# B and C convolution channels of the first layer in one 128-partition tile

## The reference

```
proj = x @ W_in.T                       # 512 z | 640 xBC | 4 dt
xp = jnp.pad(xBC, ((0, 0), (D_CONV - 1, 0), (0, 0)))
xc = conv_b + sum((xp[:, k:k + L, :] * conv_w[:, k] for k in range(D_CONV)))
xc = jax.nn.silu(xc)
x_ssm, B_ssm, C_ssm = xc[..., :512], xc[..., 512:576], xc[..., 576:]
dt = jax.nn.softplus(dt_raw + dt_bias)
A = -jnp.exp(A_log)
y = _ssd(x_ssm, dt, A, B_ssm, C_ssm) + x_ssm * D[:, None]
...                                     # rms norm of y, times silu(z), @ W_out.T
```

## Time and profile before

| | us |
|---|---|
| median of three runs | 1829.97 |
| lowest and highest run | 1828.99, 1835.95 |
| span of the profiled execution | 1829.6 |

### The profile page before, as it was taken

The page is one execution under the profiler, slowest core; times in us unless marked ns, Lnnn a source line. Parts: engine busy times, 40 slices in busy tenths (PEclk is TensorE's granted clock), DMA queues, the critical chain, the costliest instruction groups (busy, mean ns, idle before and its releaser), DMA issues. The chain is left out here.

```text
span 1829.6 us, 26010 instructions
## 1 busy us (share of the span) xinstructions
PE 1590.3 (87%) x7554; PEld 1124.3 (61%) x7554; DVE 1362.5 (74%) x3565; ACT 1149.7 (63%) x2769; POOL 756.6 (41%) x2052
## 2 busy tenths in 40 slices
PE   5799999989857889977997889878779999999987
PEld 2555657465646667766786678756645556555554
DVE  6665757572359999999999999999644466776646
ACT  3333342412148999899989998999547565665630
POOL 3504224240136776777666776777410100001000
PEclk9789999999879889999999899998999999999989
DMA  5000000000200000000000000000000000000000
GB/s 229 1 1 1 1 1 1 1 1 0 76 35 1 1 1 1 1 1 1 1 1 1 1 1 1 1 1 1 1 0 1 1 1 1 1 13 1 13 0 23
DMA packets 6717, 19.23 MB, mean 11 GB/s; under 512 B 1072, under 2 KB 4144, under 8 KB 5296
## 3 DMA queue, kind: packets, MB, share of 16 engines
q1 hardware_dynamic: 6576, 17.58, 2.6%
HBM read 15.48 MB, written 2.10 MB: 10 GB/s over the span
## 5 line engine op out<-in xcount | busy, mean ns | idle before, releaser
L1349 DVE BATCH_NORM_STATS2 r_moments<-mem_arena 128x6 f32<-128x512 f32 x576 | 382.2, 682 | 4.4 <-ACT mem_arena L1632 4.3
L1632 ACT ACTIVATE mem_arena<-mem_arena,r_shift 128x256 f32<-128x256 f32 x792 | 351.3, 514 | 32.9 <-POOL r_shift L1540 32.9
L1700 PE MATMUL r_bank<-arena,r_wT 128*128 128x256 f32 x1024 | 228.2, 381 | 7.2 <-ACT mem_arena L1632 5.5
L1700 PEld LDWEIGHTS r_bank<-arena,r_wT 128*128 128x128 f32 x1024 | 192.0, 190 | 37.1 <-issue 12.0
L1717 PE MATMUL r_bank<-ident,mem_arena 128*128 128x128 f32 x576 | 107.2, 318 | 77.4 <-DVE mem_arena L1365 77.1
L1313 DVE MAX8 r_top<-r_bank 128x8 f32<-128x256 f32 x384 | 144.0, 415 | 17.3 <-PE r_bank L1700 17.0
L2254 ACT ACTIVATE arena<-arena,e_NM 128x512 f32<-128x512 f32 (+3 forms) x256 | 134.3, 558 | 29.2 <-DVE e_NM L1942 29.2
L1717 PEld LDWEIGHTS r_bank<-ident,mem_arena 128*128 128x128 f32 x576 | 81.7, 163 | 113.0 <-DVE mem_arena L1365 100.3
L1710 PE MATMUL r_bank<-arena,ident 128*128 128x256 f32 x384 | 140.3, 452 | 3.3 <-ACT r_wT L1650 3.1
L1700 PE MATMUL r_bank<-arena,r_xnT 128*128 128x256 f32 x512 | 123.1, 402 | 19.7 <-ACT mem_arena L1632 18.3
L1942 DVE CUSTOM_DVE_ANT_0 arena<-e_banks,mask_q 128x512 f32<-128x512 f32 (+3 forms) x256 | 110.2, 485 | 28.6 <-PE e_banks L2459 28.2
(11 more groups left out here) (332 smaller groups left out, 3392.2 us busy)
## 6 DMA issues: line engine op xcount, KB each, us to landing
w<-in_w SPq DMA_DIRECT2D x3, 1024.0 KB, 14.2
out_x<-X SPq DMA_DIRECT2D x4, 512.0 KB, 2.9
X<-in_x SPq DMA_DIRECT2D x1, 1536.0 KB, 10.4
w_in<-in_w_in SPq DMA_DIRECT2D x1, 1156.0 KB, 6.4
mem_arena<-in_wq SPq DMA_DIRECT2D x1, 1024.0 KB, 17.2
mem_arena<-in_wo SPq DMA_DIRECT2D x1, 1024.0 KB, 20.8
gate<-in_gate SPq DMA_DIRECT2D x1, 1024.0 KB, 7.3
up<-in_up SPq DMA_DIRECT2D x1, 1024.0 KB, 9.3
```

What stands on the lines that cost most here:

```text
L1349: last = dve.bn_stats(moments[:, a.lane, 2 * p:2 * p + 2, :].rearrange("p two c -> p (two c)"), u[a.lane][:, 2 * p:2 * p + 2, :].rearrange ...
L1632: last = act.activation(u[a.lane][:, h, :], u[a.lane][:, h, :] if k else scores[:, h, :], ACT.Relu, bias=shift[:, a.lane, h:h + 1])
L1700: last = pe.matmul(scores[:, h, :], lhs, (G1 if a.first else G2)[:, h, i, :], start=i == 0, stop=i == 1)
```

## The change

B and C become one tile, j = 4, of 128 partitions (B on 0 to 63, C on 64 to 127), so there are `CP = 5` tiles. Projection, copy, last tap and the three VectorE taps of j = 5 disappear, together with their places in the three orders. `conv` keeps six slots. ScalarE's SiLU of the pair is done in two halves by a new function: it reads C from partitions 64 to 127 of slot 4 and writes it to partitions 0 to 63 of slot 5, then does B in place, so that the chunk loop reads what it read before. Both halves stand after `open_gate(f, 3)`; the SiLU of j = 4 used to stand ahead of it. The counts of the semaphores follow, and the fourth z projection waits for the second tile (`conv_bank(1)`, the bank ST), no longer for the sixth.

```diff
 CJ = NH0 + 2
+CP = NH0 + 1
...
-        conv_in = sb("m_conv_in", [P, CJ, S + DCONV - 1])
+        conv_in = sb("m_conv_in", [P, CP, S + DCONV - 1])
...
         def conv_bank(j):
-            return (Y, ST, CS, BC, Y, ST)[j]
+            return (Y, ST, CS, BC, Y)[j]
...
                 for j in js:
-                    n = P if j < NH0 else DS
-                    dve.wait_ge(conv_in_ready, at(b, CJ, j + 1))
+                    dve.wait_ge(conv_in_ready, at(b, CP, j + 1))
                     for k in range(DCONV - 1):
-                        last = dve.scalar_tensor_tensor(conv[0:n, j, :], conv_in[0:n, j, k:k + S], tap(j, k),
-                                                        conv[0:n, j, :], ALU.mult, ALU.add)
+                        last = dve.scalar_tensor_tensor(conv[:, j, :], conv_in[:, j, k:k + S], tap(j, k),
+                                                        conv[:, j, :], ALU.mult, ALU.add)
...
                 convolve(b, 4)
                 hide(f, 2)
-                convolve(b, 5)
                 hide(f, 3)
...
+            def bc_silu(b):
+
+                act.wait_ge(conv_ready, at(b, CP, NH0 + 1))
+                act.activation(conv[0:DS, NH0 + 1, :], conv[DS:2 * DS, NH0, :], ACT.Silu).then_inc(silu_ready, 1)
+                act.activation(conv[0:DS, NH0, :], conv[0:DS, NH0, :], ACT.Silu).then_inc(silu_ready, 1)
...
                 conv_silu(b, 0)
-                conv_columns(b, 5)
                 open_gate(f, 1)
...
                 z_silu(b, 2, 3)
-                conv_silu(b, 3, 4)
+                conv_silu(b, 3)
                 open_gate(f, 3)
-                conv_silu(b, 5)
+                bc_silu(b)
                 chunk_rows(b, 0)
...
-                    c0 = DI + j * P if j < NH0 else 2 * DI + (j - NH0) * DS
+                    c0 = DI + j * P
...
             def project_z(b, *ts):
...
-                    pe.wait_ge(conv_in_ready, at(b, CJ, t + 3))
+                    pe.wait_ge(conv_in_ready, at(b, CP, (3, 4, 5, 2)[t]))
...
                 f_pair(f, 0)
-                project_conv(b, 5)
                 f_pair(f, 1)
```

More of the change, by code:

```diff
@@ L50 @@
 _at = 0
-for _name, _n in (("dt_bias", NH0), ("A_log", NH0), ("skip", NH0), ("conv_w", CJ * DCONV), ("conv_b", CJ),
+for _name, _n in (("dt_bias", NH0), ("A_log", NH0), ("skip", NH0), ("conv_w", CP * DCONV), ("conv_b", CP),
                   ("log_beta", NHM), ("g_state", KD), ("b_state", KD), ("g_mem", 1), ("b_mem", 1),
@@ L194, in tap @@
         def tap(j, k):
-            n = P if j < NH0 else DS
-            return vec[0:n, VEC["conv_w"][0] + j * DCONV + k:VEC["conv_w"][0] + j * DCONV + k + 1]
+            return vec[:, VEC["conv_w"][0] + j * DCONV + k:VEC["conv_w"][0] + j * DCONV + k + 1]
         def heads(ap):
@@ L576, in conv_columns @@
                 for j in js:
[L577 to L581, removed]
+                    act.wait_ge(proj_done, at(b, CP, j + 1))
+                    act.activation(conv_in[:, j, DCONV - 1:], bank[conv_bank(j)][:], ACT.Copy)
+                    act.activation(conv[:, j, :], bank[conv_bank(j)][:], ACT.Identity, scale=tap(j, DCONV - 1),
+                                   bias=vec[:, VEC["conv_b"][0] + j:VEC["conv_b"][0] + j + 1]).then_inc(conv_in_ready, 1)
             def conv_silu(b, *js):
                 for j in js:
-                    n = P if j < NH0 else DS
-                    act.wait_ge(conv_ready, at(b, CJ, j + 1))
-                    act.activation(conv[0:n, j, :], conv[0:n, j, :], ACT.Silu).then_inc(silu_ready, 1)
+                    act.wait_ge(conv_ready, at(b, CP, j + 1))
+                    act.activation(conv[:, j, :], conv[:, j, :], ACT.Silu).then_inc(silu_ready, 1)
+            def bc_silu(b):
+                act.wait_ge(conv_ready, at(b, CP, NH0 + 1))
+                act.activation(conv[0:DS, NH0 + 1, :], conv[DS:2 * DS, NH0, :], ACT.Silu).then_inc(silu_ready, 1)
+                act.activation(conv[0:DS, NH0, :], conv[0:DS, NH0, :], ACT.Silu).then_inc(silu_ready, 1)
             def z_silu(b, *ts):
@@ L727, in project_conv @@
                     elif j >= 4:
-                        pe.wait_ge(conv_in_ready, at(b, CJ, j - 3))
+                        pe.wait_ge(conv_in_ready, at(b, CP, j - 3))
                     for k in range(KD):
-                        last = pe.matmul(bank[conv_bank(j)][0:n, :], w_in[:, k, c0:c0 + n], xnT[:, k, :], start=k == 0,
+                        last = pe.matmul(bank[conv_bank(j)][:], w_in[:, k, c0:c0 + P], xnT[:, k, :], start=k == 0,
                                          stop=k == KD - 1)
@@ L2741, in lay_out @@
     cw, cb = g("L0_attn_conv_w"), g("L0_attn_conv_b")
[L2742 to L2745, removed]
+    for j in range(CP):
+        vec[:, VEC["conv_w"][0] + j * DCONV:VEC["conv_w"][0] + (j + 1) * DCONV] = cw[j * P:(j + 1) * P]
+        vec[:, VEC["conv_b"][0] + j] = cb[j * P:(j + 1) * P]
     put("log_beta", rep(g("L1_attn_log_beta")))
```

## The result

| | median of all runs, us | lowest, highest | runs |
|---|---|---|---|
| before | 1828.72 | 1827.24, 1835.95 | 18 |
| changed | 1833.14 | 1830.93, 1837.54 | 18 |

The ratio is 1.0021, interval 1.0014 to 1.0027: the change costs 3.8 us (2.6 to 4.9; the two medians of the table lie 4.4 us apart). It is well inside 0.5%, on the slower side, within the range given, and five times the +0.7 us of the sum. The time of a run is about 1.8 us above its profiled span (1832.11 beside 1830.3 in the changed kernel's profile), so the profile of before stands for a run of about 1831.4, 2.7 us above that kernel's median.

The account below looks back on a forecast made before the run. Cycle 0's stretch before its chunk loop was taken as paced by VectorE, cycles 1 to 3 by TensorE. Terms -1.8 + 0 + 0.8 + 1.7 = +0.7 us on the median 1829.97 gave 1830.7 us, range 1826.2 to 1834.6.

Parts of the forecast that it names:

- Cycle 0 gains 1.8 us: Before cycle 0's chunk loop: VectorE's removed taps save 2.29 us, a second SiLU half returns 0.52; term -1.8 us.
- VectorE's taps are worth nothing in cycles 1 to 3: Cycles 1 to 3: the removed taps lie in VectorE idle time with 3.89 us to spare; term 0.
- TensorE's projection only becomes a pause: Cycles 1 to 3, before slice 1's up product: the removed 1.86 us becomes TensorE idle time awaiting `hide`; term 0.
- rival B: Cycles 0 to 3: all removed VectorE and TensorE work comes through as gain, -7.4 us, 1822.6 us; chance 0.04.
- SiLU order, +0.8: Cycles 1 to 3: two SiLU halves behind slice 3's gate delay TensorE's transposes by 0.26 us per cycle; term +0.8 us.
- Clock, +1.7 for one fall in three cycles: TensorE's new pause, cycles 1 to 3: one fall to half clock for 3.4 us, costing 1.7 us; bounds 0 and +5.1.
- Rival A: TensorE's new pause, cycles 1 to 3: the clock doesn't fall there; 1829.0 us, chance 0.22.
- C: New pause costs the clock in all three cycles: short falls 1834.1 us, chance 0.11; long falls 1844.3 us, chance 0.02.
- D: Cycle 0's chunk loop: shifted clock falls lose the 1.8 us gain, 1832.5 us, or spare 5.1, 1825.6 us; chance 0.13.

Follow-up runs that it names:

- the filled one: Changed kernel plus an unused two-step, 512-column product in TensorE's pause between gate and up product of slice 1, cycles 1 to 3: 1831.12 us, ratio 1.0004.
- the kernel with z in the pause: Changed kernel with z projections 0 and 1 moved into TensorE's pause, ahead of the up product of slice 1, in cycles 1 to 3: 1817.79 us, ratio 0.9928.

## Why the prediction was right, and where the sum was off

- *Cycle 0 gains 1.8 us.* Right in mechanism; it was 1.55 in the first profile, 0.2 less, mostly because the halves stand 0.66 apart, not 0.52. The second profiles agree: GpSimd's first chunk work starts at 50.45 and 50.55 before, at 48.90 and 49.00 after. That the gain is carried through the chunk loop can't be shown: the loop's own scatter, 2 us, is larger.
- *VectorE's taps are worth nothing in cycles 1 to 3.* Shown: with them put back those cycles take 236.98 us, as without.
- *TensorE's projection only becomes a pause.* Right: 2.58 to 2.93 us, released by `hide`, and rival B is out. The forecast was 2.14 to 2.5.
- *SiLU order, +0.8.* Right place, mis-sized. It is 0.53 us per cycle in place of 0.26, 1.6 in all (2.25 us from the up product to the transposes instead of 1.72): the term took the two halves to overlap as two SiLUs in place do, and the one that moves between partitions doesn't; without the move it is 0.26, as forecast. It came out just above the upper bound given.
- *Clock, +1.7 for one fall in three cycles.* This is what came: all seven profiles of kernels that keep the whole pause have one fall of 3.4 us, six in cycle 1 and one in cycle 2, and the seven others have none in cycles 1 to 3. Its price is right too (1.7 us, cycle 1 against the filled one). That it is a draw in each cycle by itself isn't borne out: no profile has two falls or none. Why it is just one is open. Rival A holds only for the cycles without a fall, C didn't occur.
- *D, that cycle 0 comes out otherwise.* It does, by 2 us either way, and for the kernel before as well.

Part of the agreement is luck. The forecast stands at 1830.7, the measured median at 1833.14, and D (1832.5) and C with short falls (1834.1) lie nearer to it by the number alone; C is out by its mechanism, three falls, where the traces have one. The sum also started from 1829.97, a median of three runs, where 18 runs give 1828.72. Its +0.7 is near what the profiles give for the first layer's terms (-1.55 + 2.7 = +1.15), but the whole, +3.8, lies in the range because the range was wide, and not by a term of the sum.

Cycles 1 to 3 cost 2.7 us by the profiles, where the corrected terms give 1.6 + 1.7 = 3.3 us. The wait of 0.3 to 0.6 us that the kernel before has at the same place goes into the new pause, and the start of the second projection group comes sooner; I have not split the remainder.

What the sum left out lies behind the first layer. I had let the shift pass through unchanged. In fact the entmax stage is 2.5 us longer, because 20 instructions fewer ahead of it put VectorE's stalls at other instructions; the stalls that the profile shows add up to 1.8 of it. The stretch from 345 to 622 us is 1.75 us shorter, with its mean clock at 0.91 for 0.88 and 0.89. And the falls of the clock in the last stage are worth up to 2.8 us. With the means of two profiles each: -1.55 + 2.7 - 1.75 + 2.5 + 0.4 = +2.3; the other 1.5 of the 3.8 are less than the scatter of cycle 0's chunk loop between two profiles of one kernel, and are not placed. The step that failed is the silent one, that a shift of the first layer's end is passed on as it is.

Open are why the kernel with z in the pause has a short entmax stage (675.86) although its VectorE stream is that of the changed kernel, with the same stalls in the view; what causes the stalls, and the 0.7 us of that stage that they don't cover; and which falls of the clock in the last stage follow from what.

## What to carry to other kernels

Taking instructions from an engine that waits buys only a pause; ask which engine's work can be moved into the pause, and do it in the same edit: here that turned +3.8 us into -13. Before a stage is credited with a few us, take a second profile of the unchanged kernel and compare stages between equal instructions, as some stages scatter less than the whole (the entmax stage by 0.1 us between two profiles of one kernel, the runs of the kernel by 8). Effects of 1 to 2 us can be given back further on, and only the stage shows them.

## What the runs showed of the hardware

- A ScalarE instruction that reads partitions 64 to 127 and writes 0 to 63 starts only when its neighbour has ended and holds back the next: 0.62 and 0.66 us apart, against 0.50 and 0.52 without the move, in each of cycles 1 to 3.
- A pause of TensorE of 2.6 to 2.9 us between dense products drew one fall to 1.2 GHz in three cycles, in each of seven profiles, for 3.4 us, worth 1.7. Pauses of 0.85 to 1.22 us at the same place drew none.
- VectorE has stalls of 0.17 and 0.42 us at fixed positions of its instruction stream, six of them in a row 256 instructions apart. 20 instructions more at the head, executed in idle time, put other instructions at these positions, where no stall shows, and shortened a stage of 677.7 us by 2.4.
